# A Perceiver block on one core: the output weights of cross-attention split inside the batch loop, and its projections put one place earlier

## What is computed

```python
x = x + _L0_xattn_ref(_layernorm(x), ctx_1024, mask, Wq, Wkv, Wo, qn_w, kn_w)   # 8 heads, 257 context rows per sequence
x = x + _L0_attn_ref(_layernorm(x), ...)   # q, k, v: h = x @ W, batch norm, sigmoid; A @ V @ Wo + bo
x = x + _L0_ffn_ref(_layernorm(x), ...)    # 8 experts, the best 2 for each row
```

## Time and profile before

| | us |
|---|---|
| median of 3 runs | 750.65 (749.28 to 753.72) |
| profiled execution, its own time | 752.54 |
| its span, first to last instruction | 750.8 |
| PE busy | 710.5 |
| DVE busy | 491.3 |
| ACT busy | 442.1 |
| POOL busy | 240.8 |
| mean granted PE clock, share of 2.4 GHz | 0.982 |

### The profile page before, as it was taken

The page is one execution under the profiler, slowest core; times in us unless marked ns, Lnnn a source line. Parts: engine busy times, 40 slices in busy tenths (PEclk is TensorE's granted clock), DMA queues, the critical chain, the costliest instruction groups (busy, mean ns, idle before and its releaser), DMA issues.

```text
span 750.8 us, 14081 instructions
## 1 busy us (share of the span) xinstructions
PE 710.5 (95%) x4873; PEld 590.5 (79%) x4873; DVE 491.3 (65%) x902; ACT 442.1 (59%) x958; POOL 240.8 (32%) x209
## 2 busy tenths in 40 slices
PE   4899999999999999999999989999999939999996
PEld 3677888888888888888888877888778827887874
DVE  6766766675757667757576566967467765655573
ACT  4655675675656656856666666564554435555550
POOL 1462212121212122212121125744920023555535
PEclk9999999999999999999999999999999959999999
DMA  9941121212121212121212306540124546665558
GB/s 305 98 127 42 43 86 43 85 50 75 46 79 42 84 42 84 43 83 42 84 42 85 100 1 183 180 148 10 57 85 168 171 145 217 104 107 104 109 82 326
DMA packets 59672, 75.21 MB, mean 100 GB/s; under 512 B 8784, under 2 KB 33360, under 8 KB 59632
## 3 DMA queue, kind: packets, MB, share of 16 engines
q1 hardware_dynamic: 52032, 58.16, 25.9%
q0 software_dynamic: 4720, 11.27, 8.2%
q10 hardware_dynamic: 2880, 5.24, 1.9%
HBM read 54.75 MB, written 19.92 MB: 99 GB/s over the span
## 4 chain that ended last, share of the span: by engine, by line
PE 84%; DVE 6%; DMA 4%; ACT 3%; issue 2%; POOL 1%; SPq 0%; POOLq 0%; ACTq 0%; DVEq 0%
PE pK L32 41%; PE pV L32 11%; PE pP L32 9%; PE pV L1625 5%; PE pT L1526 4%; PE pT L1714 4%; PE pS L1669 2%; PE pP L1696 2%; PE pT L1851 1%; DMA big<-x_rows,idx_x 1%; DMA fin<-total 1%; PE pT L1506 1%; PE pS L1791 1%; DVE bst L995 1%; PE pS L1874 1%
## 5 line engine op out<-in xcount | busy, mean ns | idle before, releaser
L32 PE MATMUL pK<-parts 128*128 128x512 f32 x840 | 211.3, 399 | 1.5 <-POOL parts L576 1.5
L535 POOL TENSOR_TENSOR parts<-big,parts 128x1024 fp32r<-128x1024 f32 x32 | 77.7, 2429 | 311.4 <-ACT parts L762 311.4
L32 PEld LDWEIGHTS pK<-parts 128*128 128x128 f32 x840 | 152.0, 188 | 32.3 <-POOL parts L576 2.0
L1037 DVE TENSOR_TENSOR kn<-pK,head_rs 128x512 f32<-128x512 f32 x62 | 42.9, 692 | 58.3 <-ACT head_rs L676 58.3
L32 PE MATMUL pK<-w,lhs 128*128 x276 | 70.8, 406 | 0.9 <-issue 0.6
L32 PEld LDWEIGHTS pK<-w,lhs 128*128 128x128 f32 x276 | 51.4, 192 | 12.9 <-issue 2.8
L32 PE MATMUL pP<-pT,parts 128*128 128x256 f32 x384 | 52.0, 284 | 0.0
L1452 DVE TENSOR_TENSOR w_p<-big,w_p 128x1024 fp32r<-128x1024 f32 x22 | 27.0, 1225 | 37.7 <-ACT w_p L952 37.7
L610 POOL DMA_INDIRECT big<-x_rows,idx_x x23 | 26.8, 1166 | 76.8 <-DVE idx_x L1408 60.8
L1031 DVE TENSOR_REDUCE head_ss<-sq 128x8 f32<-128x512 f32 x62 | 42.5, 685 | 13.1 <-ACT sq L670 13.1
L670 ACT ACTIVATE sq<-pK 128x512 f32<-128x512 f32 x62 | 36.9, 595 | 23.1 <-PE pK L32 23.0
(11 more groups left out here) (320 smaller groups left out, 1454.3 us busy)
## 6 DMA issues: line engine op xcount, KB each, us to landing
big<-in_ctx_dram SPq DMA_DIRECT2D x32, 512.0 KB, 3.8
total<-zero SPq DMA_DIRECT2D x32, 256.0 KB, 4.0
w_raw<-in_L_ffn_w_dram SPq DMA_DIRECT2D x16, 512.0 KB, 5.9
big<-in_L_ffn_w_dram SPq DMA_DIRECT2D x8, 512.0 KB, 4.7
fin<-total SPq DMA_DIRECT2D x8, 512.0 KB, 7.6
x_rows<-big ACTq DMA_DIRECT2D x8, 256.0 KB, 2.2
total<-big ACTq DMA_DIRECT2D x8, 256.0 KB, 2.4
big<-in_x_dram SPq DMA_DIRECT2D x1, 1536.0 KB, 9.8
```

The lines of the kernel that those rows point to most:

```text
L32: last = pe.matmul(out, lhs(a, c), rhs(b, c), start=start and c == first and n == 0, stop=stop and c == chunks - 1 and n == 2)
L535: nc.gpsimd.tensor_tensor(ctxN[:, u, LO], ctx_raw[:, u], ctxN[:, u, HI].bitcast(F32), ALU.subtract).then_inc(cn_lo, 1)
L1037: tt(heads(kn[:, t]), heads(pKV[t][:, :]), per_head(head_rs[:, t]), ALU.mult).then_inc(k_n, 1)
```

## The change

- The split weights xo_p move to the upper half of w_p (80 to 96 KB), which nothing else uses after the first batches. ACT splits their high parts behind batches 2 and 3 (two chunks each), DVE all four low parts: chunks 0 and 1 behind batch 3, 2 and 3 behind batch 28.
- Tiles 0 and 1 of the layer's output get buffers of their own, out_first, in holes of the split key weights. ACT's out_high(0) and (1) stand behind batches 28 and 29, POOL's out_low(0) and (1) behind its parts of batches 30 and 31.
- Every projection stands one place sooner on PE: 0 in batch 31, 1 and 2 ahead of the transposes in the closing batch, 3 behind them, 4 behind the closing batch and ahead of out_tile(7), 5 to 7 between the turns. ACT's out_high and DVE's out_add move with them.
- On POOL the scalings of the query weights still stand ahead of out_low(4), and the low part of those weights ahead of out_low(6).
- xT becomes two tensors, the high one at 64 KB and the low one at 32 KB. The raw weights of experts 2 and 5 change places in the order of loads and splits, since expert 5's lie where xo_p now is.

The diff, cut to what the text speaks of:

```diff
--- before.py
+++ after.py
@@ -177,12 +177,14 @@
         z = at("z", [P, C, H, BT, S], 64 * KB)
 
 
-        xo_p = parts[:, 4 * C * D:6 * C * D].rearrange("p (s c n) -> p s c n", s=2, c=C)
+        xo_p = w_p[:, 2 * C * D:4 * C * D].rearrange("p (s c n) -> p s c n", s=2, c=C)
+
+        out_first = [[at(f"out_first{t}{s}", [P, C, P], (18 + 4 * (2 * t + s)) * KB, F32R) for s in (HI, LO)] for t in range(2)]
         out_p = parts[:, 6 * C * D:7 * C * D].rearrange("p (u s c n) -> p u s c n", u=2, s=2, c=C)
         bn_k = at("bn_k", [P, 2, D], 56 * KB)
         bn_c0 = at("bn_c0", [P, D], 60 * KB)
         a_flat = at("a_flat", [P, 2 * D], 128 * KB)
-        xT = at("xT", [P, 2, C, TILES * P], 64 * KB, F32R)
+        xT = [at("xT_hi", [P, C, TILES * P], 64 * KB, F32R), at("xT_lo", [P, C, TILES * P], 32 * KB, F32R)]
         w_a = at("w_a", [P, 2, 2, C, D], 96 * KB, F32R)
         xn3 = wide[:, 0:2 * C * D].rearrange("p (t d) -> p t d", t=TILES)
         bn_vec = at("bn_vec", [P, 4, D], 128 * KB)
@@ -567,14 +573,15 @@
                     b = k * 2 + u
                     queries(b, u)
                     ctx_parts(b, u)
+            def out_low(t):
+                pool.wait_ge(oT_hi, t + 1)
+                nc.gpsimd.tensor_tensor(out_of(t, LO), qoT[:, :, t * P:(t + 1) * P],
+                                        out_of(t, HI).bitcast(F32), ALU.subtract).then_inc(oT_lo, 1)
+
             for b in (B - 2, B - 1):
                 queries(b, b % 2)
                 ctx_parts(b, b % 2)
-
-            def out_low(t):
-                pool.wait_ge(oT_hi, t + 1)
-                nc.gpsimd.tensor_tensor(out_p[:, t % 2, LO], qoT[:, :, t * P:(t + 1) * P],
-                                        out_p[:, t % 2, HI].bitcast(F32), ALU.subtract).then_inc(oT_lo, 1)
+                out_low(b - (B - 2))
 
             def bn_weight(w, c):
 
@@ -584,8 +591,7 @@
                 nc.gpsimd.tensor_tensor(raw(name)[:, c], raw(name)[:, c], bn_ac[w][0],
                                         ALU.mult).then_inc(w_scaled, 1)
 
-            low_part("xo", XO_ORDER[:1])
-            for t in range(TILES):
+            for t in range(2, TILES):
                 if t == C:
                     for c in range(C):
                         bn_weight(0, c)
@@ -790,17 +796,16 @@
                         act.wait_ge(p_rt, tile)
                         act.activation(pT_rem[0:3 * B, :], pV1[0:3 * B, 0:G * P], ACT.Copy).then_inc(p_rh, 1)
                 if not main:
-                    out_high(3)
-                    ln_root(TILES)
+                    ln_root(TILES + 1)
+                    out_high(4)
                     bn_root(0)
                 if main:
                     keys_copy(b + 1)
                 if nxt:
                     k_square(b + 1, 0)
                 if main and not nxt:
-                    high_part("xo", XO_ORDER)
                     act.wait_ge(pc_mm, (b - 1) * 2 + 2)
-                    out_high(0)
+                    out_high(2)
 
                 if prev:
                     if r == 1 and not first:
@@ -823,34 +828,36 @@
                 act.activation(bn_of[w][:, 3, :], bn_of[w][:, 3, :], ACT.Exp, scale=-0.5).then_inc(bn_rs, 1)
 
             def out_high(t):
-                if t >= 2:
+                if t >= 4:
                     act.wait_ge(xo_mm, t - 1)
-                act.activation(out_p[:, t % 2, HI], qoT[:, :, t * P:(t + 1) * P], ACT.Copy).then_inc(oT_hi, 1)
+                act.activation(out_of(t, HI), qoT[:, :, t * P:(t + 1) * P], ACT.Copy).then_inc(oT_hi, 1)
 
             for r in range(1, BT):
                 batch(0, r, first=r == 1)
+                if r >= 2:
+                    high_part("xo", (2 * r - 4, 2 * r - 3))
             with act.Fori(1, TILES - 1) as k:
                 for r in range(BT):
                     batch(k, r)
             for r in range(BT):
                 batch(TILES - 1, r, nxt=r < BT - 1)
-            out_high(1)
+                if r < 2:
+                    out_high(r)
+            out_high(3)
             batch(TILES, 0, main=False, nxt=False)
 
 
-            out_high(4)
-            ln_root(TILES + 1)
             out_high(5)
+            out_high(6)
             for t in range(2, TILES + 2):
                 if t < TILES:
                     ln_root(TILES + t)
                 if t == 2:
                     high_part("aq")
-                ln_high(TILES + t - 2, xT[:, HI, :, (t - 2) * P:(t - 1) * P])
-                if t + 4 < TILES:
-                    if t + 5 == TILES:
-                        act.wait_ge(o_out, TILES)
-                    out_high(t + 4)
+                ln_high(TILES + t - 2, xT[HI][:, :, (t - 2) * P:(t - 1) * P])
+                if t == 2:
+                    act.wait_ge(o_out, TILES)
+                    out_high(TILES - 1)
                 if t == 3:
                     bn_root(1)
                     act.wait_ge(zeroed, 16 * B)
@@ -1147,6 +1154,8 @@
                         pS[:, :, 0:M], ALU.mult, ALU.add).then_inc(sc_m, 1)
                     dve.wait_ge(sc_m, b)
                     nc.vector.tensor_reduce(neg_max[:, :], s_m[:, :, 0:M], AX.X, ALU.max, negate=True).then_inc(sc_max, 1)
+                if not main:
+                    out_add(0)
                 if nxt:
                     ctx_low(b + 1, 1 - u)
                 if prev:
@@ -1164,7 +1173,7 @@
                 if main:
                     k_sum(b, 1)
                 if not main:
-                    out_add(0)
+                    out_add(1)
                 if main:
                     k_norm(b, 1, reused=not first)
                 if r == 1 and not first:
@@ -1173,18 +1182,13 @@
                     dve.wait_ge(p_hi, b)
                     tt(pT[:, LO], pP[:, :, :], pT[:, HI].bitcast(F32), ALU.subtract).then_inc(p_lo, 1)
                 if not main:
-                    out_add(1)
                     ln_norm(TILES, x_all[:, 0])
+                    out_add(2)
                     bn_scale(0)
                 if main:
                     dve.wait_ge(k_t, b * MT + 1)
                     ts(kT[:, :, M - 1:M], kT_rem[:, :, bass.ds(b, 1)], 1.0, None, ALU.mult).then_inc(k_rem, 1)
                     keys_copy(b + 1)
-                if main and not nxt:
-                    for c in XO_ORDER[1:]:
-                        dve.wait_ge(w_hi, high_count("xo", c))
-                        tt(xo_p[:, LO, c], raw("xo")[:, c], xo_p[:, HI, c].bitcast(F32),
-                           ALU.subtract).then_inc(w_lo[JOB["xo"]], 1)
                 if nxt:
                     k_sum(b + 1, 0)
 
@@ -1210,26 +1214,34 @@
                 dve.wait_ge(x1_add, t + 1)
                 ln_stats(TILES + t, x_all[:, t])
 
+            def output_weight_low(chunks):
+                for c in chunks:
+                    dve.wait_ge(w_hi, high_count("xo", c))
+                    tt(xo_p[:, LO, c], raw("xo")[:, c], xo_p[:, HI, c].bitcast(F32),
+                       ALU.subtract).then_inc(w_lo[JOB["xo"]], 1)
+
             dve.wait_ge(not_mask, 1)
             for r in range(1, BT):
                 batch(0, r, first=r == 1)
+            output_weight_low((0, 1))
             with dve.Fori(1, TILES - 1) as k:
                 for r in range(BT):
                     batch(k, r)
             for r in range(BT):
                 batch(TILES - 1, r, nxt=r < BT - 1)
+                if r == 0:
+                    output_weight_low((2, 3))
             batch(TILES, 0, main=False, nxt=False)
-            out_add(2)
             ln_norm(TILES + 1, x_all[:, 1])
+            out_add(3)
             bn_shift(0)
-            out_add(3)
             out_copy(TILES - 1)
 
 
             for t in range(2, TILES + 2):
                 if t < TILES:
                     ln_norm(TILES + t, x_all[:, t])
-                ln_low(TILES + t - 2, xT[:, LO, :, (t - 2) * P:(t - 1) * P], xT[:, HI, :, (t - 2) * P:(t - 1) * P])
+                ln_low(TILES + t - 2, xT[LO][:, :, (t - 2) * P:(t - 1) * P], xT[HI][:, :, (t - 2) * P:(t - 1) * P])
                 if t + 2 < TILES:
                     out_add(t + 2)
                 if t == 4:
@@ -1633,7 +1646,7 @@
                     pe.wait_ge(w_lo[JOB["xo"]], C)
                 if t >= 2:
                     pe.wait_ge(x1_add, t - 1)
-                split_products(pe, pKV[t % 2][:, :], tile_of(out_p, t % 2), weight(xo_p), C).then_inc(xo_mm, 1)
+                split_products(pe, pKV[t % 2][:, :], lambda s, c: out_of(t, s)[:, c, :], weight(xo_p), C).then_inc(xo_mm, 1)
 
             def z_product(n):
 
@@ -1682,9 +1695,12 @@
                     pe.wait_ge(k_n, b * MT + 1)
                     pe.wait_ge(ctx_lo, b * MT + 3)
                     split_products(pe, pK0[:, :], ctx_rows(1 - u, 0), wk, C - 1, stop=False)
+                if main and not nxt:
+                    pe.wait_ge(k_n, b * MT + 1)
+                    project(0)
                 if not main:
-                    project(0)
                     project(1)
```

(15 more changed lines are left out.)

28 lines of the change are left out of this document (16 added, 12 removed).

## The result

| | before | changed |
|---|---|---|
| median of 9 runs, us | 750.08 (749.25 to 753.72) | 756.74 (755.0 to 758.27) |
| profiled execution, us (span) | 752.54 (750.8) | 757.74 (755.9) |
| mean granted clock of the profiled execution | 0.982 | 0.980 |

The account below looks back on a forecast made before the run. TensorE (PE), busy 95% of the span, was taken as the bound. The terms 3.6 (tail), 0.2 (weights' split) and 1.6 (clock) sum to +5.4 us: 757.9 for the profiled execution, 756.0 for the median; range 751.4 to 758.7.

Parts of the forecast that it names:

- Until the fifth projection: End of cross-attention on PE: filled gaps bring PE to 464.5 with one more projection done, 3.6 us better.
- The small new wait: Before batch 31's 24 products on PE: they start at 449.2, 0.7 us late, after the probabilities' transposes and DVE's subtraction.
- The fifth projection: project(4) on PE: stalls 5.7 us, from 464.5 to 470.2, because POOL's four scalings stand ahead of out_low(4).
- The tail: From project(4) to self-attention's third product: waits of 0.6 at project(6), 1.3 and 0.2 at turns; +3.6 us there.
- Turn 13: LayerNorm turn on PE, numbered among 8 to 15: waits 1.3 us for the low part made from turn 11.
- turn 15: Last LayerNorm turn on PE: stands behind DVE's shift of the key vectors and waits 0.2 us more.
- The weights' split: Work added in batches 2, 3 and 28, felt in batch 4: +0.2 us, bounds 0 (slack holds) and 0.8.
- The clock: PE's granted clock falls in the stall, project(4) runs at half speed: +1.6 us, bounds 0 and 2.8.
- the first: Rival at project(4): the stall comes but the clock holds; +3.8 us, 754.4; chance 0.20.
- The second: Rival: waits at project(6) and turns 13 and 15 (2.1 us) vanish; +3.3, or +1.7 without clock loss; chance 0.20.
- The third: Rival in POOL's queue: out_low(4) comes in time, no stall or clock fall; -2.1 us, 748.5; chance 0.04.
- The fourth: Rival: vectors or POOL a microsecond later, clock low longer, batch 4 at its bound; +8, 758.7; chance 0.06.

Follow-up runs that it names:

- scale_later: Changed kernel with POOL's four scalings of the query weights moved behind out_low(4); 750.67 us, ratio 0.998 to the kernel before.
- order_back: Changed kernel with out_tile(7) again ahead of project(4) and projections 4 to 7 behind turns 8 to 11 on PE; 755.94 us, ratio 1.0059 to before.
- warm_again: Changed kernel with 24 unused products of 128x512 filling the stall ahead of project(4), second timing; 755.04 us, ratio 1.0044 to the kernel before.
- turns_cover: both_later with project(7) behind turn 11 instead of turn 10; 748.61 us, ratio 0.9962 to the kernel before.
- weights_only: Kernel before with only Wo's split moved, xT in two tensors and experts 2 and 5 exchanged; 752.6 us, ratio 1.0012 to before.
- weights_again: weights_only run once more, with a second profile; 751.53 us, ratio 1.0003 to the kernel before.
- after_again: The changed kernel itself, unaltered, timed in the same rounds as warm_again; 757.26 us, ratio 1.0073 to the kernel before.
- both_later: Changed kernel with POOL's scalings behind out_low(4) and the query weights' low part behind out_low(6); 749.41 us, ratio 0.9969 to the kernel before.
- products_cover: turns_cover with the products of xT one turn sooner on PE; 752.2 us, ratio 0.9999 to the kernel before.

## Why the prediction was right

By its own steps:

- *Until the fifth projection.* PE was to be ready at 464.5; it was at 464.75. The small new wait was to make the products of batch 31 start at 449.2; they started at 449.20 (a wait of 0.34 is seen one piece sooner, before the keys' transposes). project(1) was to come at 452.7: 452.79.
- *The fifth projection.* Forecast: a stall of 5.7 us to 470.2, released by POOL behind the scalings. Measured: 5.67, to 470.42; scalings from 463.55 to 468.69. That the order of POOL is the cause is shown by scale_later, in which one move takes the stall away. The remark that out_tile had covered the scalings is right as far as order_back goes: with it ahead again project(4) does not wait.
- *The tail.* Waits of 0.6, 1.3 and 0.2 were summed. project(6) waited under 0.2: its turn ran at 482.54 and it started at 483.07. The clock is not the reason, for in warm_again, at full clock, it waits as little (turn at 480.90, start at 481.45). What was sized wrong is POOL's low part of the weights, taken as 5.7 us from before; in both kernels it was through after 5.22 (476.50 to 481.72 in the changed one). Turn 13 waited 1.28. The third product is as late as the first, so turn 15 added nothing. The explanation of turn 13 (three bare turns, and ACT's copy and DVE's subtraction behind each other) was incomplete, as turns_cover shows: VectorE's other work ahead of that subtraction is what counts.
- *The weights' split.* +0.2 forecast. Batch 4 measured 4.93 us from its first product to the transposes, 4.90 before. Two rows of PE and VectorE's context low parts in the changed kernel, then the transposes in the kernel before, which go with the earlier trace rows:

```profile
102.01 5.09 PE L32 MATMUL pK<-parts 128*128 128x512 f32 x21
106.94 0.60 PE L1712 MATMUL pP<-ident,prob 128*128 128x128 f32 x4
104.05 1.28 DVE L1033 TENSOR_TENSOR parts<-pT,parts 128x512 fp32r<-128x512 f32 x2
```

```profile
106.59 0.60 PE L1696 MATMUL pP<-ident,prob 128*128 128x128 f32 x4
```

  The slack held, but only just: the first low part is ready at about 104.7 (half of the 1.28), and PE takes it at 104.8 (102.01 plus 2.79). PE reached the keys of batch 31 at 441.52, for 441.67 before, so nothing was lost on the way; weights_only and weights_again find no difference in time either.
- *The clock.* +1.6 forecast; 4.32 less 2.79 is 1.53 in the first profile, about 1.9 in the paired profiles and 2.2 by their medians. The Trainium skill (TensorE: Matmul & The Clock Gate, "What's actually happening") is borne out as to the sign: with nothing to do the engine went back to the low clock, and work brought it up again. Which gap costs the clock the quoted sentence doesn't tell: 1.48 and 0.57 us in the profile of before left it at 1.00, and 1.52 and 0.53 in the two profiles of weights_only and weights_again did not.

Sum: 5.31 at the first xT product and 5.2 for the profiled execution, against +5.4. Some of that closeness is luck. The forecast counted 0.4 us too much at project(6), 0.2 at turn 15 and 0.2 for the weights; against that project(4) started 0.2 later than forecast, and between turn 8 and the first xT product three pieces ran 0.1 to 0.3 longer each. The medians of the first rounds differ by 6.7, those of after_again's rounds by 5.5 (757.26 for 751.73). What makes the first 6.7 isn't shown; the nine times of before spread over 4.5 us.

The rivals: the first (the clock holds) is what the filled stall gave, +3.3 by warm_again's median against +3.8. The second, by which the waits at project(6), turn 13 and turn 15 vanish, came in part: turn 13's wait of 1.28 stayed, project(6)'s shrank to 0.2 and turn 15's is not there. project(6)'s is smaller because of POOL's shorter low part, not because DVE and ACT catch up in the stall; for turn 15 the reason isn't shown. The third, whose condition is that out_low(4) comes in time, was made by hand: scale_later gave -0.95 and both_later -2.2 by the medians (-2.1 forecast for it). The fourth did not come.

## What to carry to other kernels

When work is moved sooner on the engine that bounds, walk each queue that feeds it and ask what stands ahead of the feeding instruction there, and what that in turn waits for: here four scalings that hang on a load stood ahead of a split whose input was ready, and 3.6 us of filled gaps turned into 5.67 us of stall. An in-order queue should have its instructions in the order in which their inputs come and their outputs are wanted. A gap on TensorE costs more than its length if the clock falls in it or just behind it: 1.5 to 2.2 us for the long one here, but 1.7 also for one of 2.10 us in products_cover, and 1.1 to 1.2 for the pair of 1.52 and 0.53 in the weights' kernels. Short gaps aren't safe by being short.

## What the hardware showed unexpectedly

- The clock falls in one program at different distances from PE's stop: about 5.2 us after it in one execution of the changed kernel, about 2.5 in another, with the same work on both sides.
- It also fell behind gaps of 1.52 and 0.53 us, in two profiles of one kernel, and held in the profile of the kernel before with 1.48 and 0.57. The spread of times between executions goes with the mean clock: in the 18 executions of before beside weights_only, 0.979 for 753.6 us, 0.983 and more for 750.8.
- A tiny VectorE operation on 128x2, which reads two operands, takes 0.97 to 1.02 us in the eleven profiles in which POOL subtracts 128x512 at that moment, and 0.16 in the three in which it doesn't (before, weights_only, weights_again). In all eleven it ends 0.01 to 0.02 us behind POOL's operation, as if it had to wait for it: at 445.88 and 445.87 in these rows of the changed kernel. The reciprocal ahead of it, which reads one operand, took 0.17 during the same subtraction. That the second operand makes the difference is a guess; no run changes it alone.

```profile
444.70 0.17 DVE L1166 RECIPROCAL p_inv<-p_den 128x2 f32<-128x2 f32 x1
444.90 0.98 DVE L1168 SCALAR_TENSOR_TENSOR p_scale<-neg_max,p_inv 128x2 f32<-128x2 f32 x1
```

```profile
444.56 1.31 POOL L578 TENSOR_TENSOR out_first<-qoT,out_first 128x512 fp32r<-128x512 f32 x1
```

  It makes the keys late for which PE waits 0.34. Nothing is lost by it in the end: PE's products behind start at 449.20, when the low part of the probabilities is there, and that comes by another chain.
